# A recurrent mixture of experts behind local attention on one core: spectra of two vocabulary halves at once, the start reordered, and the output projection computed feature-major

## The reference

```python
# 1. tokens: 89 embedding features, 39 spectral ones
word   = emb_table[ids]                                    # (16, 512, 89)
spec   = |rfft(window * frames(one_hot(ids)))|             # 64-point frames, hop 64: 9 frames, 33 frequencies,
feats  = spec[frame = t * 9 // 512]                        #   for each of 16 vocabulary entries
h      = concat(word, feats @ proj_w + proj_b)             # (16, 512, 128)
# 2. attention of 8 heads on layernorm(h): 64 summary tokens with 7 keys each, 448 others
#    with a window of 17 keys and their summary token; then
h      = h + attn @ W_out + b_out
# 3. two of 8 experts per token, chosen by a router on layernorm(h); every expert is an LSTM over
#    the 16 sequences (the step axis), for all 512 positions, with the inputs masked to its tokens
gates  = x_masked @ Wi + hid @ Wh + b;  c = sig(f)*c + sig(i)*tanh(g);  hid = sig(o)*tanh(c)
h      = h + sum_k w_k * (hid_k @ Wo + bo)
```

## Time and profile before

| | |
|---|---|
| median of 3 runs | 1867.98 us (1867.66 to 1868.47) |
| the profiled execution: time | 1867.89 us |
| its span, first to last instruction | 1866.0 us |
| PE busy | 1740.3 us (93%) |
| DVE busy | 1542.1 us (83%) |
| ACT busy | 997.0 us (53%) |
| mean granted TensorE clock | 0.958 |

### The profile page before, as it was taken

One profiled execution on the slowest core, in us unless ns is written; L12 is line 12 of the kernel. 1 busy time (PEld: TensorE's weight loads), 2 busy tenths in 40 slices (PEclk: granted clock), 3 DMA queues, 4 the chain that ended last, 5 costly groups with the idle time before them and its releaser, 6 DMA issues.

```text
span 1866.0 us, 25899 instructions
## 1 busy us (share of the span) xinstructions
PE 1740.3 (93%) x9898; PEld 852.3 (46%) x9898; DVE 1542.1 (83%) x2417; ACT 997.0 (53%) x1114; POOL 38.0 (2%) x42
## 2 busy tenths in 40 slices
PE   4447899999999999999999999999999999999998
PEld 2223444444444444544444444444444444444443
DVE  2649897988889888898988889898888988889865
ACT  4225645646465554646546464565646556464544
POOL 0000000000000000000000000000000000000000
PEclk9768999999999999999999999999999999999999
DMA  3123221313123131221323223131322314232121
GB/s 117 21 36 83 64 64 52 74 41 82 47 53 74 44 79 42 64 68 40 74 56 70 43 63 64 49 77 39 78 53 52 75 45 71 49 63 68 45 63 37
DMA packets 203905, 110.95 MB, mean 59 GB/s; under 512 B 125642, under 2 KB 184892, under 8 KB 203782
## 3 DMA queue, kind: packets, MB, share of 16 engines
q1 hardware_dynamic: 203782, 109.30, 25.8%
HBM read 89.84 MB, written 4.74 MB: 51 GB/s over the span
## 4 chain that ended last, share of the span: by engine, by line
PE 61%; DVE 26%; issue 7%; ACT 4%; DMA 1%; SPq 1%; POOL 0%; DVEq 0%; ACTq 0%
PE gates L528 45%; PE yp L534 4%; DVE tmp L1024 3%; DVE tmp L1003 2%; DVE xm L996 2%; DVE Hs L1008 2%; DVE C L1028 2%; DVE tmp L1018 2%; DVE tmp L1039 2%; ACT tmp L677 2%; PE FB L488 2%; PE FA L469 2%; PE FB L487 2%; PE FA L454 2%; DVE z L1043 1%
## 5 line engine op out<-in xcount | busy, mean ns | idle before, releaser
L670 ACT ACTIVATE tmp<-gates,bias_sb 128x1024 f32<-128x1024 f32 x504 | 559.7, 1111 | 571.4 <-PE gates L528 570.1
L528 PE MATMUL gates<-xm,wi_sb 128*128 128x512 f16 x3024 | 759.1, 389 | 14.2 <-DVE xm L996 9.5
L528 PE MATMUL gates<-Hs,wh_sb 128*128 128x512 f16 x2880 | 708.1, 382 | 0.0
L528 PEld LDWEIGHTS gates<-xm,wi_sb 128*128 128x128 f16 x3024 | 294.5, 100 | 410.9 <-issue 117.0
L528 PEld LDWEIGHTS gates<-Hs,wh_sb 128*128 128x128 f16 x2880 | 284.8, 99 | 349.1 <-issue 16.3
L677 ACT ACTIVATE tmp<-C 128x1024 f32<-128x1024 f32 x128 | 135.2, 1056 | 149.6 <-DVE C L1028 145.7
L1003 DVE SCALAR_TENSOR_TENSOR tmp<-tmp 128x1024 f32<-128x1024 f32 x128 | 156.5, 1223 | 58.6 <-ACT tmp L677 56.7
L1018 DVE SCALAR_TENSOR_TENSOR tmp<-tmp 128x1024 f32<-128x1024 f32 x120 | 145.2, 1210 | 64.3 <-ACT tmp L670 64.3
L1024 DVE SCALAR_TENSOR_TENSOR tmp<-tmp,C 128x1024 f32<-128x1024 f32 x120 | 145.7, 1214 | 39.4 <-ACT tmp L670 38.8
L996 DVE TENSOR_TENSOR xm<-xs,masks 128x2048 f16<-128x2048 f16 x128 | 155.7, 1217 | 11.8 <-DMA masks<-mask_scratch 11.8
L1008 DVE SCALAR_TENSOR_TENSOR Hs<-tmp,Hs 128x1024 f16<-128x1024 f32 x120 | 146.7, 1222 | 16.3 <-ACT Hs L681 16.3
(11 more groups left out here) (155 smaller groups left out, 1231.0 us busy)
## 6 DMA issues: line engine op xcount, KB each, us to landing
masks<-mask_scratch SPq DMA_DIRECT2D x128, 256.0 KB, 5.2
roww<-mw_scratch SPq DMA_DIRECT2D x128, 256.0 KB, 3.5
rowk<-mask_scratch SPq DMA_DIRECT2D x128, 128.0 KB, 2.9
diag<-pr SPq DMA_DIRECT2D x64, 112.0 KB, 3.2
diag<-vwin SPq DMA_DIRECT2D x64, 112.0 KB, 3.2
out_dram<-h SPq DMA_DIRECT2D x16, 256.0 KB, 2.2
C<-in_wi SPq DMA_DIRECT2D x1, 2048.0 KB, 10.4
C<-in_wh SPq DMA_DIRECT2D x1, 2048.0 KB, 15.1
```

The lines of the kernel that those rows point to most:

```text
L528: last = mm(gates[:, slot, k * SEQ:(k + 1) * SEQ], w, v, start=(i < K), stop=(i >= len(seq) - K))
L670: A(tmp[:, gate_at(gate, e), :], gates[:, (n - 1) % 2, :], ACT.Tanh, bias=bias_sb[:, e, gate:gate + 1], scale=UNSCALE).then_inc(s_tanh, 1)
```

## The change

Four parts:

- **Spectra.** Entries 0 to 7 of the vocabulary stand on partitions 0 to 32, entries 8 to 15 on partitions 64 to 96. The DFT matrix lies between zeros, so that two pairs of matmuls fill both in one accumulation; three chunks in place of six, each with two buffers for the squares. The DFT matrix is loaded over ScalarE's queue, behind which ScalarE takes a root of one column ahead of everything. The adds stand ahead of the wait for the constants. The projection takes 8 matmuls on 97 partitions.
- **First front.** The ids of batch 0 are loaded right behind the weights, and `table` from `encA` in SBUF. The high halves of `wi` follow `h` of batch 0 and those of `wh` its summary; the low halves of `wi` follow its `xn`, those of `wh` its weights (slot 23).
- **Second front.** The front of batch 0 runs by `run_front` with s = -1, so that slots -8 to -1 of batch 1 run in its slots 24 to 31, ahead of step 0. The first two mask loads stand at slots 26 and 27, ahead of SP's store of the weights' rows.
- **Projection.** `attn` moves to slot 15. At slot 16 one matmul computes the projection feature-major into FA, ScalarE copies it with the bias into `xnT`, and at slot 17 four transposes make it token-major.

```diff
-    PE_AT = dict(... values=15, proj=17, x2T=20, logits=21, maskT=25)
+    PE_AT = dict(... values=15, proj=16, projT=17, x2T=20, logits=21, maskT=25)
-    ACT_AT = dict(... feature=12, x2T=20, choice=22, maskT=25)
+    ACT_AT = dict(... feature=12, proj=16, x2T=20, choice=22, maskT=25)
-    DVE_AT = dict(... attn=16, ...)
+    DVE_AT = dict(... attn=15, ...)
@@ run_front
-            if s == 0 and t == 0:
-                for u in range(-EARLY, 0):
-                    front(u, 1)
@@ sync
             load(fid, frame_ids, s_stft_in)
-            load(dft_sb, dft.rearrange("n c f -> n (c f)"), s_stft_in)
             load(vrow, vocab_rows, s_stft_in)
+            sp.wait_ge(s_dz, 2)
+            for g in range(2):
+                load(pw_sb[g * GP:g * GP + NFREQ, :].rearrange("f (v o) -> f v o", v=VH),
+                     proj_w.rearrange("(f v) o -> f v o", v=VOCAB)[:, g * VH:(g + 1) * VH, :], s_pw_in)
...
             load(wo_sb[:, :, :], wo.rearrange("e i n -> i e n"), s_wo_load)
+            load(ids, x_ids[0:1, :].to_broadcast([VOCAB, SEQ]), S["ids"])
             sp.wait_ge(s_enc_sb, 2)
+            load(table[ENC0:ENC0 + NFR, D_EMB:D], encA[0:NFR, :], S["enc"])
             load(enc_dram[0:P, :], encA, s_enc_out)
...
             for t in range(-EARLY, NG * E):
-                front(t, 0)
-            mask_in(0, 0)
-            mask_in(0, 1)
+                run_front(front, t, -1)
+                if t in (MASKS_AT, MASKS_AT + 1):
+                    mask_in(0, t - MASKS_AT)
@@ tensor
+                pe.wait_ge(s_oh64, 2 * (c + 1))
                 for r in range(2):
-                    for v in (HI, LO):
-                        last = mm(gates[0:NFREQ, c % 2, r * SEQ:r * SEQ + SC], dft16[:, v, r * NFREQ:(r + 1) * NFREQ],
-                                  onehot64[:, c * SC:(c + 1) * SC], start=(v == HI), stop=(v == LO))
+                    for g in range(2):
+                        at = GP if g == 0 else 0
+                        for v in (HI, LO):
+                            last = mm(gates[0:NP2, c % 2, r * SEQ:r * SEQ + SC], dftz[:, v, r, at:at + NP2],
+                                      onehot64[:, g * VH * NBJ + c * SC:g * VH * NBJ + (c + 1) * SC],
+                                      start=(g == 0 and v == HI), stop=(g == 1 and v == LO))
...
                 if t == PE_AT["proj"]:
                     pe.wait_ge(S["attn"], b1)
+                    mm(FA[:, 1, :], wout_sb[:, :], attn[:, :], start=True, stop=True).then_inc(S["projT"], 1)
+                if t == PE_AT["projT"]:
+                    pe.wait_ge(S["projS"], b1)
                     for i in range(TILES):
-                        mm(FB[:, i * D:(i + 1) * D], attn[:, i * P:(i + 1) * P], wout_sb[:, :], start=True, stop=False)
-                        last = mm(FB[:, i * D:(i + 1) * D], ones1[:, :], bout_sb[:, :], start=False, stop=True)
+                        last = nc.tensor.transpose(FB[:, i * D:(i + 1) * D], xnT[:, i * P:(i + 1) * P], ident[:, :])
                     last.then_inc(S["proj"], 1)
@@ scalar
+            act.dma_start(dft_sb, dft.rearrange("n c f -> n (c f)")).then_inc(s_dft_in, 16)
+            act.wait_ge(s_pad, 1)
+            A(red[:, 0:1], kf[:, 0:1], ACT.Sqrt)
...
+                if t == ACT_AT["proj"]:
+                    act.wait_ge(S["projT"], b1)
+                    A(xnT[:, :], FA[:, 1, :], ACT.Identity, bias=bout_sb[:, 0:1]).then_inc(S["projS"], 1)
...
-            split_w_hi(wi_st, wi_sb, 1.0, s_wi_load)
...
-            split_w_hi(wh_st, wh_sb, 0.5, s_wh_load)
             for t in range(-EARLY, NG * E):
-                front(t, 0)
+                run_front(front, t, -1)
+                if t == ACT_AT["h"]:
+                    split_w_hi(wi_st, wi_sb, 1.0, s_wi_load)
+                if t == ACT_AT["summary"]:
+                    split_w_hi(wh_st, wh_sb, 0.5, s_wh_load)
@@ vector
+            V.memset(dftz_flat, 0.0).then_inc(s_dz, 1)
+            V.memset(pw_sb[32:GP, :], 0.0).then_inc(s_dz, 1)
...
             for t in range(-EARLY, NG * E):
-                front(t, 0, 0)
-                if t == DVE_AT["moments"]:
-                    split_w_lo(0, 4)
-                if t == DVE_AT["w_max"]:
-                    split_w_lo(4, 6)
+                run_front(lambda u, b: front(u, b, b % 2), t, -1)
+                if t == DVE_AT["xn"]:
+                    split_w_lo(0, 3)
...
+                if t == DVE_AT["weights"]:
+                    split_w_lo(3, 6)
```

More of the change, by code:

```diff
@@ L56, in lm_tower_kernel @@
     SP_AT = dict(ids=-8, qbd=1, vz=5, rows=25, wrow=28)
-    PE_AT = dict(emb=-5, xT=-2, qkv=-1, summary=2, window=4, feature=10, values=15, proj=17, x2T=20,
+    PE_AT = dict(emb=-5, xT=-2, qkv=-1, summary=2, window=4, feature=10, values=15, proj=16, projT=17, x2T=20,
                  logits=21, maskT=25)
-    ACT_AT = dict(h=-5, xT=-2, qkv=-1, split=0, summary=4, window=7, pr_hi=11, feature=12, x2T=20,
+    ACT_AT = dict(h=-5, xT=-2, qkv=-1, split=0, summary=4, window=7, pr_hi=11, feature=12, proj=16, x2T=20,
                   choice=22, maskT=25)
     DVE_AT = dict(onehot=-6, moments=-4, xn=-3, pw=0, q_lo=0, kv_lo=1, v_win=2, w_max=3, s_max=5, s_sub=6, w_sum=7,
-                  w_out=8, s_sum=9, s_norm=10, f_max=11, p_lo=12, p_T=13, f_sum=14, f_part=14, attn=16,
+                  w_out=8, s_sum=9, s_norm=10, f_max=11, p_lo=12, p_T=13, f_sum=14, f_part=14, attn=15,
                   moments2=18, xn2=19, x_lo=21, choice1=22, choice2=22, weights=23)
@@ L193, in lm_tower_kernel @@
         SC = 384
-        NSC = VOCAB * NBJ // SC
-        sq = tmp[0:NFREQ, 0:2, 0:SC]
+        NSC = VH * NBJ // SC
+        sq = [tmp[0:NP2, 0:2, b * SEQ:b * SEQ + SC] for b in range(2)]
         enc_dram = nc.dram_tensor("enc_scratch", (NBJ, D_ENC), f32, kind="Internal").ap()
@@ L206, in lm_tower_kernel @@
         s_stft_in = sem("s_stft_in")
+        s_dft_in = sem("s_dft_in")
+        s_pw_in = sem("s_pw_in")
+        s_pad = sem("s_pad")
+        s_dz = sem("s_dz")
         s_zero = sem("s_zero")
@@ L247, in lm_tower_kernel @@
             pw sw mw dw ew rw iw ow owr ow_c pf sf mf df ef rf if_ uf S mS dS eS rS iS prT O of0 of1
-            khi vhi qhi qlo klo vlo pn phi plo cf attn proj h2 bnst2 bnag2 veps2 rstd2 xn2 x2p xhi x32 xlo lgp lg m1 eq1 ix1 im1 k1 l2 m2
+            khi vhi qhi qlo klo vlo pn phi plo cf attn projT projS proj h2 bnst2 bnag2 veps2 rstd2 xn2 x2p xhi x32 xlo lgp lg m1 eq1 ix1 im1 k1 l2 m2
             eq2 ix2 im2 k2 dd ed sd w0 w1 wa wb wt mwc mwp mrow wT mout wout ybo"""
@@ L284, in lm_tower_kernel @@
             (rw_sb[:, :], router_w), (rb_sb[:, :], row(router_b).to_broadcast([P, E])), (bo_sb[WT0:WT0 + E, :], bo),
[L285 removed]
+            (bout_sb[:, :], col(b_out)), (ident[:, :], ident_dram), (hones[:, :], head_ones), (band_sb[:, :], band),
             (par_sb[:, :], parity), (m8_sb[:, :], expert_m8), (vcol[:, :], vocab_col),
@@ L315, in front @@
             def front(t, b):
-                if t == SP_AT["ids"]:
+                if t == SP_AT["ids"] and not is_zero(b):
                     sp_ids(b)
@@ L338, in sp_ids @@
             def sp_ids(b):
[L339 to L342, removed]
+                sp.wait_ge(S["onehot"], b)
+                sp.wait_ge(S["emb"], b)
+                sp.wait_ge(S["ef"], b)
                 sp.wait_ge(s_enc_out, 32)
@@ L413, in _ @@
                     pe.wait_ge(s_sq, 2 * (c - 1))
-                if c % 2 == 0:
-                    pe.wait_ge(s_oh64, c // 2 + 1)
+                pe.wait_ge(s_oh64, 2 * (c + 1))
                 for r in range(2):
-                    for v in (HI, LO):
-                        last = mm(gates[0:NFREQ, c % 2, r * SEQ:r * SEQ + SC], dft16[:, v, r * NFREQ:(r + 1) * NFREQ],
-                                  onehot64[:, c * SC:(c + 1) * SC], start=(v == HI), stop=(v == LO))
+                    for g in range(2):
[4 more added lines that the diff above has]
+                                      start=(g == 0 and v == HI), stop=(g == 1 and v == LO))
                     last.then_inc(s_dft, 1)
             pe.wait_ge(s_mag, 1)
-            for v in range(VOCAB):
+            pe.wait_ge(s_pw_in, 48)
+            for v in range(VH):
                 last = mm(FA[0:D_ENC, 0, 0:NBJ], pw_sb[:, v * D_ENC:(v + 1) * D_ENC], mag[:, v * NBJ:(v + 1) * NBJ],
-                          start=(v == 0), stop=(v == VOCAB - 1))
+                          start=(v == 0), stop=(v == VH - 1))
             last.then_inc(s_encT, 1)
@@ L756, in _ @@
             TS(bias_sb[:, :, O:O + 1], bias_sb[:, :, O:O + 1], 0.5, None, ALU.mult).then_inc(s_prep, 1)
-            for c in range(NSC):
-                dve.wait_ge(s_sq, 2 * c + 2)
-                TT(mag[:, c * SC:(c + 1) * SC], sq[:, 0, :], sq[:, 1, :], ALU.add).then_inc(s_msq, 1)
             def split_w_lo(a, b):
```

74 lines of the change are left out of this document (42 added, 32 removed).

## The result

The changed kernel takes **1794.77 us** (median of 4 runs, 1793.76 to 1796.47), the kernel before 1868.22 in the same comparison (4 runs, 1867.66 to 1870.3). The ratio is 0.9606, with a 95% interval of 0.9589 to 0.9622: 73.5 us less. The forecast was 1792, in a range of 1778 to 1823.

What follows compares the result with a forecast made beforehand. The prediction took TensorE to bound the steps and the order of waits to decide the start and step 0. Savings of 50 + 12.8 + 5.6 + 7.5 = 75.9 us from 1868 gave 1792 us, range 1778 to 1823.

Steps and rivals of the forecast that it cites:

- The bound: In the steps, a microsecond less on TensorE (busy 109.65 of 111 us) is a microsecond less of time, if VectorE keeps up.
- The projection in the steps, 50 us: In 14 steps, the new projection saves a net 3.55 us each, 50 us in all; range 39 to 57.
- the bare stall: In each step, TensorE waits 1.7 us for `attn` behind `unit_y`, no longer hidden behind a gate unit.
- the copy's cover: In each step, ScalarE's new copy is ready 0.7 us before TensorE asks for it.
- the new stall ahead of x2T: In each step, TensorE waits 0.55 us for layernorm two's `xn2`.
- Does the clock stay up: In the steps, TensorE's granted clock no longer falls behind the projection, despite the new stall and four more transposes.
- The forecast's ground in the earlier trace: At 197 to 211 us, TensorE idles 5 of 14 us among gate units, yet the granted clock is 0.98.
- The spectra, 12.8 us: In the start, the first `emb` matmul begins at 28.4 us, not 41.23: 12.8 us off, range 10 to 19.
- Rival 2: In the start, small loads overtake the weights: 6 us more off, 1786 us in all; chance 0.10.
- The weight splits, 5.6 us: In batch 0's front, 3.5 us from moving low halves and 2.1 from the projection come off; range 4 to 7.
- The mask wait, 7.5 us: Before step 0's third mask, batch 1's qkv comes sooner, at 118.7 instead of 126.15: 7.5 us off, range 0 to 9.
- Rival 3: In step 0, gate unit 0 behind qkv sets the pace, so 7.5 us come back: 1799 us; chance 0.08.

Runs made afterwards that it cites:

- e4: The changed kernel with the new projection matmul and its transposes one slot later each, at slots 17 and 18: 1772.45 us.
- e1: The kernel before with only the new projection part of the change: 1819.6 us.
- e3: The kernel before with only `attn` moved from slot 16 to slot 15, the sixteen small projection matmuls kept: 1822.0 us.
- e5: The kernel before without the eight bias matmuls of the projection (b_out left out), the gap ahead kept: 1810.8 us.
- e11: The changed kernel with batch 0's ids loaded ahead of the weights, the copy of `encA` into `table` still on SP's queue: 1794.73 us, one execution.
- e7: The changed kernel with batch 0's ids loaded ahead of the weights and the copy of `encA` into `table` on ScalarE's queue: 1790.61 us.
- e8: The changed kernel with the three low halves of `wi` behind batch 0's moments, ahead of `xn`, in place of behind it: 1799.3 us.
- e12: The changed kernel with `wi`'s high halves ahead of the encodings and its low halves behind batch 0's moments: 1797.59 us, one execution.
- e6: The changed kernel with slots -8 to -1 of batch 1 back in step 0, as before the change: 1802.62 us.
- e10: The kernel before with `attn` at slot 15 and each projection bias matmul done twice, making 24 small matmuls: 1858.68 us.

## Why the prediction was right, point by point

**The bound.** Right. TensorE's microseconds in a step were the time's: e4 took 1.5 us off a step (107.4 to 105.9) and 22.3 us off the run.

**The projection in the steps, 50 us.** Measured 48.5, and 49.2 by itself in e1. The stretch is 8.18 us (8.2 forecast), the bare stall 1.60 (1.7), the copy's cover 0.8 (0.7), the new stall ahead of x2T 0.55 (0.55), and a step 107.4 (107.4).

**Does the clock stay up.** Right in what it forecast, and not right in why. The step "what came before each fall was the projection itself: small fp32 matmuls" left out the idle time ahead of them. e3 has the same sixteen without the gap, and nine of 14 falls are gone; e5 has the gap with eight that take 1.00 us, and all are gone. In the kernel before it was both together. That changes what the edit is worth: moving `attn` by one slot, one number in a table, gave 46.8 us, the new shape of the projection another 2.4 where it stands (hardly more than the runs of one kernel differ by), and its place in e4 22.3 more. The conclusion for the kernel after survived because its stretch, 2.6 us, is shorter than all in the table that brought a fall. The forecast's ground in the earlier trace rows was thin, though, and there luck had a part: just ahead of that window the same trace has a granted clock of 0.57 (194 to 198 us), behind a wait for a tanh that ended at 194.50 and had lasted 2.1 us, not much longer than the new stall. With four more transposes in a step the granted clock is 1.00, so what the Trainium skill ("TensorE: Matmul & The Clock Gate", Part 4: PE-mode transpose) says of them cost nothing in these places.

**The spectra, 12.8 us.** Measured 11.8. The encodings were ready at 21.25 (20.5 to 22), and the ids held `emb` behind `wo`, as forecast. The mis-sized term is the time of that landing: SP issues `wo` at 14.34 and not at 13.25, as its instruction for `wh` lasts 3.17 us where it had lasted 2.24, and everything behind it moved by that microsecond. Rival 2, small loads that overtake, didn't happen on that queue; e11 shows the queueing and e7 what it costs.

**The weight splits, 5.6 us.** Measured 7.2, just outside its range of 4 to 7. VectorE's part was worth more: `emb` to `xn` took 10.8 us before and 5.5 after, 5.3 off where 3.5 were counted. The missing 1.9 is rstd, 2.92 before and 1.01 after, which the sum took as fixed. e8 and e12 show that both parts are real: the low halves cost 4.5 us there, and the long rstd comes back when a split is under way. The projection gave 1.9 (2.1).

**The mask wait, 7.5 us.** Measured 7.7: `emb` at 91.30 is 5.1 behind VectorE's coming free (5.3 forecast), and qkv 8.3 behind it (8.3). Rival 3, gate unit 0 as the pace, didn't happen, and e6 has the gain from the other side (7.9).

**What the sum lacked.** Step 0 gave 1.2 us back between the third mask and the first gate unit of step 1. Its cause is open, and it is one trace against one: the four runs of the kernel after differ by 2.7 us, and e6's trace has 73.4 us in the same stretch. These 1.2, the microsecond of `wo` and 1.5 in the steps, against 1.6 more from the splits and 0.2 from the mask wait, make 74.0 of 75.9.

## What to carry to other kernels

Look at what TensorE does in the microseconds ahead of a fall of the clock as one stretch, gap and small matmuls together: here taking away either was enough for most of the time, and the cheaper one was a single slot number. A stall that an edit leaves bare on the busiest engine should be tried one unit of work later before it is accepted: here that was worth 22 us, nearly a third of the whole change. In the start, ask of each small load what is ahead of it on its queue, and not only when its data is ready.

## What the hardware showed

**POOL waits out VectorE's instruction.** Its rstd, four columns, took 1.01 us with VectorE idle or starting later, and otherwise as long as the VectorE instruction under way required. In the kernel after, the front of batch 0 and the step shown above:

```profile
75.90 0.69 DVE L1113 TENSOR_SCALAR wo_sb<-wo_sb 128x1024 f32<-128x1024 f32 x1
76.07 1.38 POOL L1143 TENSOR_TENSOR rstd<-veps,mhalf 128x4 f32<-128x4 f32 x1 [41.20 <-DVE veps L961]
...
363.04 1.22 DVE L1052 SCALAR_TENSOR_TENSOR tmp<-tmp,C 128x1024 f32<-128x1024 f32 x1
363.21 1.91 POOL L1143 TENSOR_TENSOR rstd<-veps,mhalf 128x4 f32<-128x4 f32 x1 [77.05 <-DVE veps L961]
```

Each time rstd ends 0.86 us after VectorE's instruction does (77.45 - 76.59; 365.12 - 364.26), and 0.88 in the start of the kernel before (48.50 - 47.62). The other way round the rows differ. A memset of 3584 columns on POOL held VectorE's one-hot up in e12 (1.06 us in place of 0.47, to 0.27 us behind the memset's end), but rstd held nothing up in e8, where VectorE's three low halves begin 0.15 us after it and take 4.56 us as ever (4.55 in e12):

```profile
26.38 3.08 POOL L1135 MEMSET diag<- 128x3584 f32 x1 [25.40 <-PE FA L443]
28.67 1.06 DVE L820 TENSOR_SCALAR rows<-prod,vcol 16x512 f32<-16x512 int32 x1 [11.28 <-DMA prod<-in_x_ids]
...
33.77 1.01 POOL L1143 TENSOR_TENSOR rstd<-veps,mhalf 128x4 f32<-128x4 f32 x1 [9.87 <-DVE veps L831]
33.92 4.56 DVE L797 SCALAR_TENSOR_TENSOR wi_sb<-C,wi_sb 128x2048 f16<-128x2048 f32 x3 [0.30 <-ACT wi_sb L734]
```

The first two rows are e12's, the others e8's. The Trainium skill ("Trainium Architecture — The Big Picture", What this means for kernel authors) says that of the engines' ways into SBUF only the port pair of these two contends, and that it is "an exclusive lock (not a bandwidth split)". The rows agree where POOL waits and at the memset; that rstd holds such a lock for its whole 1.01 us, e8's rows do not show.

**Small matmuls of two kinds in turn are dear.** Eight fp32 instructions of 128 columns took 1.00 us back to back (e5), and sixteen, two with `wout_sb` and two of one row in turn, 3.22 to 3.43. The single row alone is not what costs: in e10 eight more one-row instructions, each behind others of one row, add 0.9 us (4.11 against 3.22). That the turns from one kind to the other cost the rest is what this points to; no run isolates it.

**TensorE can be busy throughout and the clock falls** (e10's window: busy 10.00 of 10.00 us, granted 0.83).
